# A fused attention and feed-forward kernel: first weight strips fetched as float32 on the sync queue, three steps reordered

## The reference

```python
x = x + _layernorm(_L0_attn_ref(_layernorm(x, axis=-1), L0_attn_W_q, L0_attn_W_kv, L0_attn_W_o), axis=-1)
x = x + _layernorm(_L0_ffn_ref(_layernorm(x, axis=-1), L0_ffn_W, L0_ffn_b, L0_ffn_lora_A, L0_ffn_lora_B, L0_ffn_gate_w, L0_ffn_gate_b), axis=-1)
```

## Time and profile before

| | us |
|---|---|
| median of 3 runs | 1017.05 (1016.85 to 1020.64) |
| profiled execution | 1017.06 |
| its slowest core (core 6), first to last instruction | 1015.1 (the eight cores: 1008.6 to 1015.1) |
| PE busy / DVE / ACT / POOL | 979.7 / 588.5 / 342.4 / 54.8 |
| by stage: projections / output product / feed-forward | to 525 / 525 to 748 / 748 to 1015 |

### The profile page before, as it was taken

The page is one execution under the profiler, slowest core; times in us unless marked ns, Lnnn a source line. Parts: engine busy times, 40 slices in busy tenths (PEclk is TensorE's granted clock), DMA queues, the critical chain, the costliest instruction groups (busy, mean ns, idle before and its releaser), DMA issues.

```text
span 1015.1 us, 14019 instructions; the slowest of 8 cores (1008.6 to 1015.1 us)
## 1 busy us (share of the span) xinstructions
PE 979.7 (97%) x5072; PEld 468.3 (46%) x5072; DVE 588.5 (58%) x846; ACT 342.4 (34%) x573; POOL 54.8 (5%) x106
## 2 busy tenths in 40 slices
PE   3989999999999999999999999999998999999996
PEld 2444444444444444444444444444444444444442
DVE  3134765455554456555467777666675656557565
ACT  5256666766667755656330000000000000000001
POOL 5000000000000000000001000000100000000000
PEclk9999999999999999999999999999998999999999
DMA  9995545565565222220085878877985233132222
GB/s 133 168 164 91 87 86 110 104 108 87 87 115 104 63 42 42 42 37 7 21 296 116 174 153 154 155 149 147 175 155 176 77 111 123 65 125 97 91 104 83
DMA packets 65667, 112.22 MB, mean 111 GB/s; under 512 B 37184, under 2 KB 45376, under 8 KB 63040
## 3 DMA queue, kind: packets, MB, share of 16 engines
q0 software_dynamic: 14688, 51.42, 32.9%
q1 hardware_dynamic: 50912, 59.91, 19.3%
HBM read 120.79 MB, written 33.55 MB: 152 GB/s over the span
## 4 chain that ended last, share of the span: by engine, by line
PE 89%; DMA 6%; DVE 2%; issue 1%; ACT 1%; DVEq 1%; SPq 0%; POOL 0%; ACTq 0%; POOLq 0%
PE PS L357 40%; PE PS L634 21%; PE PS L819 20%; DMA XT<-xt 4%; PE PS L291 3%; PE PS L771 1%; PE PS L315 1%; PE PS L826 1%; PE PS L396 1%; DMA XT<-wos 1%; DMA XT<-bias 1%; DMA WK<-wkv 1%; ACT WK L258 0%; DVEq L81 0%; SPq L695 0%
## 5 line engine op out<-in xcount | busy, mean ns | idle before, releaser
L357 PE MATMUL PS<-XT,WK 128*128 128x512 bf16 x2048 | 482.6, 380 | 3.2 <-DMA XT<-xt 3.2
L357 PEld LDWEIGHTS PS<-XT,WK 128*128 128x128 bf16 x2048 | 196.1, 98 | 220.0 <-issue 5.8
L634 PE MATMUL PS<-XT,VH 128*128 128x512 bf16 x1024 | 221.5, 379 | 1.3 <-DMA XT<-wos 1.3
L819 PE MATMUL PS<-WK,VH 128*128 128x512 bf16 x896 | 205.1, 381 | 0.0
L634 PEld LDWEIGHTS PS<-XT,VH 128*128 128x128 bf16 x1024 | 100.1, 98 | 122.3 <-issue 1.7
L819 PEld LDWEIGHTS PS<-WK,VH 128*128 128x128 bf16 x896 | 86.9, 98 | 101.3 <-issue 2.1
L389 DVE TENSOR_TENSOR WK<-WK 128x1024 bf16<-128x1024 bf16 x60 | 41.5, 692 | 151.6 <-ACT WK L381 147.6
L646 ACT ACTIVATE SM<-SM 128x1 f32<-128x1 f32 x48 | 14.2, 295 | 270.0 <-DVE SM L682 108.0
L273 ACT ACTIVATE WK<-PS 128x512 bf16<-128x512 f32 x120 | 70.4, 592 | 61.8 <-PE PS L291 60.4
L835 DVE TENSOR_TENSOR XT<-PS,XT 128x1024 f32<-128x1024 f32 x31 | 38.0, 1224 | 57.7 <-PE PS L802 51.2
L381 ACT ACTIVATE WK<-PS 128x1024 bf16<-128x1024 f32 x60 | 61.4, 1024 | 29.1 <-PE PS L357 25.7
(11 more groups left out here) (77 smaller groups left out, 600.0 us busy)
## 6 DMA issues: line engine op xcount, KB each, us to landing
out<-XT SPq DMA_DIRECT2D x15, 1024.0 KB, 4.8
WK<-wkv POOLq DMA_DIRECT2D x16, 512.0 KB, 6.4
WK<-wq POOLq DMA_DIRECT2D x16, 512.0 KB, 6.2
WK<-wot POOLq DMA_DIRECT2D x16, 512.0 KB, 8.4
wos<-VH SPq DMA_DIRECT2D x32, 256.0 KB, 8.6
XT<-wos SPq DMA_DIRECT2D x4, 2048.0 KB, 9.9
WK<-x POOLq DMA_DIRECT2D x16, 512.0 KB, 7.9
x1s<-WK SPq DMA_DIRECT2D x16, 512.0 KB, 4.6
```

The lines of the kernel that those rows point to most:

```text
L357: return e.matmul(bank(bk + r), WF[s % 3][:, c * 256 + r * 128:c * 256 + (r + 1) * 128], XT[:, b * 8192 + c * 512:b * 8192 + (c + 1) * 512 ...
L634: return e.matmul(bank(bk), VH[:, c * 2048 + t * 128:c * 2048 + (t + 1) * 128], XT[:, nn * 8192 + c * 512:nn * 8192 + (c + 1) * 512], star ...
L819: pe.do(lambda e, c=c: e.matmul(bank(bk), VH[:, c * 2048 + t * 128:c * 2048 + (t + 1) * 128], wchunk(c, nn * 512, (nn + 1) * 512), start=( ...
```

## The change

The first four strips are fetched as float32, by SP, into a region of `VH` that is not yet used (`RAWF`); `center` reads the float32 strip and writes bfloat16 to `RAW`. POOL waits for the third strip's landing before it issues any x. Strip ("w",2,1) is fetched behind x block 2 rather than ahead of it; its centring moves from block 2 to block 3 (k = 1), its folds from k = 1 and 2 to k = 2 and 3, and the centring of ("w",2,0) from k = 2 to k = 3 of block 2. In stage 2 the fourth and fifth early group change places. At the start of stage 3 chunks 14 and 15, the bias and three residual tiles are issued as soon as the last matmul of stage 2 is done, ahead of the store and the transposition of tile 15 on SP's queue, and `lora_turn(1)` is emitted before the first bias additions and norm.

```diff
--- before.py
+++ after.py
@@ -128,6 +128,7 @@
     WK = nc.alloc_sbuf_tensor("WK", [128, 39936], BF16)
     XTF = XT.bitcast(F32)
     WKF = WK.bitcast(F32)
+    VHF = VH.bitcast(F32)
 
     PHIT = nc.alloc_sbuf_tensor("PHIT", [HD, HD], BF16)
     PSI = nc.alloc_sbuf_tensor("PSI", [HD, HD], BF16)
@@ -141,6 +142,7 @@
     KT = WK[:, 20480:24576]
     QT = WK[:, 24576:28672]
     KT2 = VH[:, 10 * 2048:12 * 2048]
+    RAWF = [VHF[:, i * 2048:(i + 1) * 2048] for i in range(4)]
     KC = WK[:, 28672:32768]
     SQ2 = [WK[:, 32768 + i * 1536:32768 + i * 1536 + 1024] for i in range(2)]
     SQS = [WK[:, 33792 + i * 1536:33792 + i * 1536 + 512] for i in range(2)]
@@ -223,6 +225,12 @@
     raw_landed = {}
     raw_free = [None] * 4
 
+
+    l_first = [Landing(nc, "first%d" % i) for i in range(4)]
+    for k, (_, s, a) in enumerate(raw_jobs[:4]):
+        src = wkv_d if s == 0 else wq_d
+        raw_landed[raw_jobs[k]] = l_first[k].start(sp, RAWF[k], src.ap()[a * 128:(a + 1) * 128, :])
+
     def raw_load(job):
         kind, s, a = job
         i = raw_slot[job]
@@ -255,7 +263,8 @@
         k = ncent[0] % 2
         ncent[0] += 1
         act.wait(raw_landed[job])
-        t_sum = act.mark(lambda e: e.activation(RAW[i], RAW[i], AF.Identity, accum_out=SUM[k]))
+        src = RAWF[i] if job in raw_jobs[:4] else RAW[i]
+        t_sum = act.mark(lambda e: e.activation(RAW[i], src, AF.Identity, accum_out=SUM[k]))
         dve.wait(t_sum)
         dve.do(lambda e: e.tensor_scalar_mul(NMEAN[k], SUM[k], -1.0 / D))
         dve.drain()
@@ -466,20 +475,19 @@
             for fn, p, k in pieces.pop(0):
                 fn(p, k)
 
-    for job in raw_jobs[:4]:
-        raw_load(job)
+    first = raw_jobs[:4]
+    pool.wait(raw_landed[first[2]])
     for b in range(2):
         xt_load(b)
 
-    first = raw_jobs[:4]
     center(first[0])
     for k, job in enumerate(first[:3]):
         center(first[k + 1])
         for g in range(4):
             fold_w(job, g, act if g % 2 == 0 else dve)
     raw_load(("w", 2, 0))
+    xt_load(2)
     raw_load(("w", 2, 1))
-    xt_load(2)
     xt_load(3)
     sp.wait(xt_landed[0][-1])
     t_bones = l_const[1].start(sp, BONES[:, :], bones_d.ap())
@@ -514,17 +522,19 @@
             normalize(i0 - 2)
         for k in range(1, n):
             part(i0, k)
-            if strips:
+            if k > 1 and strips:
                 strips.pop(0)()
             part(i1, k - 1)
-            if strips:
+            if k > 1 and strips:
                 strips.pop(0)()
             if b >= 1 and k == 1:
                 norm(i1 - 2)
                 invert(i1 - 2)
                 normalize(i1 - 2)
-            if b == 2 and k >= 2:
-                center(("w", 2, k - 2))
+            if b == 2 and k == 3:
+                center(("w", 2, 0))
+            if b == 3 and k == 1:
+                center(("w", 2, 1))
         evacuate(i0)
         square(i0)
         if b == 2:
@@ -695,6 +705,18 @@
         sp.do(lambda e: e.dma_start_transpose(dst, XN).then_inc(l_xnt.sem, 16))
         xnt_ready[t] = (l_xnt.name, l_xnt.sem, l_xnt.count)
 
+
+    l_bias = Landing(nc, "bias")
+    l_x1r = [Landing(nc, "x1r%d" % i) for i in range(3)]
+    l_out = [Landing(nc, "out%d" % i) for i in range(3)]
+    x1r_landed = {}
+    x1r_free = [None] * 3
+    out_stored = [None] * 3
+
+    def x1r_load(t):
+        sp.wait(x1_stored[t], x1r_free[t % 3])
+        x1r_landed[t] = l_x1r[t % 3].start(sp, X1R[t % 3], x1s_d.ap()[t * 128:(t + 1) * 128, :])
+
     early = list(range(14))
     late = [14, 15]
     every = list(range(16))
@@ -707,7 +729,7 @@
     queue_pieces(last)
     while pieces:
         long_piece()
-    for t, nn in ((0, 1), (0, 2), (0, 3), (1, 0)):
+    for t, nn in ((0, 1), (0, 2), (1, 0), (0, 3)):
         out_mm(t, nn, early)
     pool.wait(vh_ready[15], slot_done[last], norm_tok[last % 2], inv_tok[last])
     x_load(0)
@@ -733,32 +755,18 @@
             t_agw = l_agw.start(pool, AGW, agw_d.ap())
         if t == 15:
             t_bbt = l_bbt.start(pool, BBT, bbt_d.ap())
+
+            pool.wait(y_tok[(15, 3)])
+            w_load(14)
+            w_load(15)
+            sp.wait(y_tok[(15, 3)])
+            t_bias = l_bias.start(sp, BIAS, bias_d.ap())
+            for k in range(3):
+                x1r_load(k)
         attn_norm(t)
         next_norm(t)
         if t + 1 < NT and t >= 1:
             x_load(t + 1)
-    t_out = y_tok[(15, 3)]
-
-
-    l_bias = Landing(nc, "bias")
-    l_x1r = [Landing(nc, "x1r%d" % i) for i in range(3)]
-    l_out = [Landing(nc, "out%d" % i) for i in range(3)]
-    pool.wait(t_out)
-    w_load(14)
-    w_load(15)
-    sp.wait(t_out)
-    t_bias = l_bias.start(sp, BIAS, bias_d.ap())
-    x1r_landed = {}
-    x1r_free = [None] * 3
-    out_stored = [None] * 3
-
-    def x1r_load(t):
-        sp.wait(x1_stored[t], x1r_free[t % 3])
-        x1r_landed[t] = l_x1r[t % 3].start(sp, X1R[t % 3], x1s_d.ap()[t * 128:(t + 1) * 128, :])
-
-    for t in range(3):
-        x1r_load(t)
-
     xat_ready = {}
     xat_mm = {}
 
@@ -901,11 +909,11 @@
     ffn_mm(1, 0, every)
     for nn in range(4):
         lora_mm(0, nn)
+    lora_turn(1)
     ffn_half(0, 0)
     ffn_half(0, 1)
     ffn_norm(0)
     x1r_load(3)
-    lora_turn(1)
     for t in range(1, NT):
         for nn in range(4):
             if t == 1:
```

## The result

The changed kernel takes 1025.88 us (1025.24 to 1027.21, 6 runs) where the kernel before took 1017.48 beside it: a ratio of 1.008, 95% interval 1.0061 to 1.0099. It is slower by 8.4 us; 1014.9 was predicted, with a range that ended at 1019.

What follows compares the result with a forecast made beforehand. PE was taken to bound the kernel (89% of the chain, DMA 6%). On core 6, 1015.1 + 1.2 - 1.3 - 2.1 gave a 1012.9 us span, plus 2.0 for profiled time: 1014.9 us, range 1010 to 1019.

Steps and rivals of the forecast that it cites:

- bank order and `lora_turn(1)`: Output product and feed-forward: weights wait gone, -1.3 us; copy wait and slow matmuls gone, -7.1; new DVE wait, +2.1.
- strip order: Stage 1: block 2 lands one strip earlier, both x waits go, block 3's part starts 2.5 us earlier.
- float32 fetch and GpSimd's wait: Start of stage 1: float32 strips land faster, 1.0 us gained; POOL's wait costs nothing, the fourth strip being in flight.
- centring moved to block 3: Stage 1, block 3: two new PE waits, 3.0 us for the first fold and 1.65 before slot 8's norm.
- early loads: Start of stage 3: bias and residual loads delay chunk 15 by 4.5 us, making PE wait 2.9 us.
- new wait for DVE: Feed-forward: PE reaches tile 2's transposition before DVE's chain ends and waits 2.1 us, once.
- the lost cover: Start of stage 1: if the fourth strip does not cover POOL's wait, x's whole stream is 2 us later.
- rival B: Stage 1: no strip lands earlier, or POOL's wait leaves a 1 us hole; 1015.9 to 1016.9 us; chance 0.12.
- Chunk 15: Feed-forward's late group: chunk 15 lands 4.5 us later against 1.6 of slack, so PE waits 2.9 us.
- C: Clock falls behind new waits of about 3 us, 2.9 us each: 1017.8 us with one, 1020.7 with both; chance 0.18.
- slot 8: Stage 1, block 3: x gains of 3.5 us against new waits of 3.0 and 1.65 make it 1.2 us later.

Runs made afterwards that it cites:

- turn_bank: Kernel before with only the output product's bank order and `lora_turn(1)` ahead of tile 0's norm; ratio 1.0012.
- turn_bank_order: turn_bank plus strip ("w",2,1) fetched behind x block 2; 1012.8 us, ratio 0.9967 against the kernel before.
- only_f32: turn_bank_order plus the float32 fetch on SP and GpSimd's wait for the third strip; median 1020.3 us, ratio 1.0013 against the kernel before.
- only_fold: turn_bank_order plus strip ("w",2,1) centred in block 3 at k = 1, folded at k = 2 and 3; ratio 1.0010 against the kernel before.
- only_loads: turn_bank_order plus chunks 14, 15, bias and three residual tiles issued ahead of tile 15's store; ratio 0.9997 against the kernel before.
- f32_wait1: only_f32 with GpSimd waiting for the first strip rather than the third; ratio 0.9963 against the kernel before.
- loads_back: Changed kernel with chunks 14, 15, bias and residual tiles issued as before, `lora_turn(1)` still early; 1021.6 us.
- no_pool_wait: Changed kernel without GpSimd's wait for the third strip; 1026.9 us.
- best: turn_bank_order plus early `BONES`, ("w",3,0) centred at k = 3 of block 3, chunks and bias issued after tile 15's bank group 0, earlier `lora_head(2)`; 1006.15 us.

## Why the prediction was wrong

The terms of the sum beside what the runs gave, in us. Each measured time is a difference of two ratios, taken on 1017 us, and carries an interval of 2 to 3 us either way; the last two columns are differences of the profiled means.

| term | forecast | measured | output product starts | stage 3 |
|---|---|---|---|---|
| bank order and `lora_turn(1)` (turn_bank) | -6.3 | +1.2 | -0.1 | -0.7 |
| strip order (turn_bank_order) | -2.5 | -4.6 | -2.7 | -0.2 |
| float32 fetch and GpSimd's wait (only_f32) | -1.0 | +4.7 | +2.7 | -0.3 |
| centring moved to block 3 (only_fold) | +4.65 | +4.4 | +4.9 | -0.4 |
| early loads (only_loads) | +2.9 | +3.1 | 0.0 | +4.0 |

The forecasts add up to -2.2, the measured times to +8.8; the whole change cost 8.1 by its ratio. Two terms failed, the first and the third, and the clock, which stands in no row, is in the measured columns of all.

*Bank order and `lora_turn(1)`: the mechanism right, the gain wrong.* The wait for the reloaded weights went, as said. The new wait for DVE was named too (2.1; 2.2 to 2.5 on most cores, up to 4.6), but 6.3 us were booked for the two parts, and turn_bank gains nothing. The sum took the 2.9 us of slow matmuls as gone with the old wait; on six of eight cores slow matmuls came back behind the new one. The 6.3 were also booked on the one core that had lost most by the old wait (4.2 us and the slow stretch; cores 0, 1, 3, 4 and 7 had waited 3.1 to 3.3), while the metric is the slowest of eight.

*The fetch and GpSimd's wait: wrong.* The step said: no cost, "the fourth still in flight", and 1.0 us gained. By stage 1 of only_f32 it costs 2.7 us, by its time about 4.7. I set one strip's 3.4 us against "under 2" from issue to packets, and left out that a landing is told after the last packets and the issue comes after that: on core 5 it is over 3 us from the third strip's last packets to the first of x, and the windows show two of them empty. On the even cores the cover held, nearly. My own text had the price of the lost cover (2 us) and rival B had "a hole of 1 us"; both gave it too little weight and too small a size.

*`BONES`: the step that is missing.* SP waits for block 0's last DMA before it issues `BONES`, and the row with its 8.1 us to landing stood among mine, read only for how queues share. A late block 0 is passed on to the first norm, and so is a PE that gets there early. The prediction followed x to blocks 2 and 3 and never asked what else hangs on block 0; the trace of the kernel before had the wait on four cores, core 5's of 1.5 us among them, and I looked at core 6 alone.

*The centring moved to block 3: right.* 3.0 and 1.65 us were forecast, 2.9 and 1.4 measured on core 5, the same in only_fold. This was the largest part of the loss and was in the sum; what was not is the clock behind it.

*Strip order: right.* 2.5 us forecast, 2.7 measured at the output product; the 4.6 by the times is not told apart from either.

*Chunk 15: right on core 5, by its size in part luck.* Wait 2.9 forecast and measured; on core 5 chunk 15 landed 15.0 us after its issue, where 10.4 had been on core 6, and that is the 4.5 us assumed. Over the cores the wait was 0 to 3.7 us, on core 6, for which it was forecast, 0.5.

*The clock: the rival that decided.* C was given 0.18 as something that happens to a forecast otherwise right, once on the slowest core, at 2.9 us a fall. Six cores have five or six waits of 1.3 to 4.2 us that are new or longer, cores 4 and 6 three and four, and the time is that of the slowest: the cores other than 6 have one to four falls behind them, core 5 four, at some 1.6 us each, 6.5 us in all. So a fall was priced too high and their number far too low. C also counted only waits of "about 3 us", and the clock fell behind 2.4 us on core 5.

*Together.* For core 6 alone the sum is close: the output product starts 1.4 us later (1.2 forecast for slot 8), stage 2 is 1.5 shorter (1.3), stage 3 is 4.0 shorter (2.1), and the span is 1011.2 against 1012.9. That is in part luck: 2.1 us of waiting for `BONES` were not in the sum, and the wait for chunk 15 was 0.5 rather than 2.9. The step from one core to the metric is where most of the number was lost: seven cores ended behind core 6, core 0, which was said to end below it, 7.7 us behind.

What stays open: why the third strip lands later on the odd cores and x's first packets come later still (first x DMA landed at 22.9, 21.5, 23.6, 24.1 us on cores 1, 3, 5, 7, and at 19.6 to 21.5 on the even ones), and whether turn_bank_order gains more than the two waits it removes; a lower number of clock falls in stage 1 would do it (two cores of turn_bank had one, none of turn_bank_order), which was only seen, not tested.

## What to carry to other kernels

A queue that is made to wait for a landing is empty for the time from the last packets to the notice, the issue and the first packets of the next transfer; that has to be covered by work already queued. Here one strip of 3.4 us did not cover it on the odd cores and three did (waiting for the first of four rather than the third was worth 0.5%, some of which the long core of only_f32 may hold); two were not tried. When a PE-bound kernel on eight cores is given small waits in exchange for others, count each at its length plus the slow stretch that can follow it, on the core that is hit most often, not on the one you looked at; and read the waits of all eight cores before the change, as one that is absent on your core (`BONES` here) may be on others. Before a load is moved, look at which matmul frees its region: here some 10 us earlier than the wait that stood in the code (an estimate: 48 matmuls of 0.216 us).

## What the runs showed of the hardware that was not expected

The clock falls behind shorter waits than the kernel before suggested: there behind 3.1 us and more, in the changed kernel behind 2.3 to 2.5 us and in turn_bank behind 2.2, on some cores and not on others with the same wait (2.2 us: cores 3, 5 and 6 of turn_bank fell, 1 and 7 did not). In the changed kernel, on core 5, just before the last of the windows above:

```profile
792.00:796.00 4.00, 1.55 (x9) 0.71 (x8) 3.11 (x11) 0.58 (x2) 0.00 (x0) 0.98 0.97 279
```

In eight of the fourteen profiled runs one or two cores stood once in stage 2, between 578 and 618 us, for 0.6 to 5.9 us of PE. In only_f32 it was core 4, whose DVE waited for the landing of a transposition, with PE behind it:

```profile
580.76 0.81 DVE L690 TENSOR_SCALAR WK<-WK,SM 128x2048 bf16<-128x2048 bf16 x1 [15.15 <-DMA VH<-WK]
...
587.66 2.72 PE L640 MATMUL PS<-XT,VH 128*128 128x512 bf16 x6 [5.88 <-DVE WK L674]
```

It costs that core 9 us with the clock behind it. It would explain why that kernel's runs scatter (1014.3 to 1022.5 us), and the three slower runs of turn_bank_order, but only the profiled runs have a trace. It is seen with the float32 fetch (5.2 us in loads_back, 4.1 in no_pool_wait) and without it (3.3 in only_fold), and none of f32_wait1's six runs or best's four has a core far behind the others; whether any part of the change makes it more likely is not shown. Why that transposition is late was not found.
